# A softplus sum moved from VectorE to TensorE in a fused convolution and selective-scan kernel

## The reference

```python
xh = silu(causal_conv_k2(xh, conv_w, conv_b))
x_dbl = xh @ W_x                      # 8 columns for dt, 16 for B, 16 for C
dt = softplus(dt_low @ W_dt + b_dt)   # L x 256
h = exp(dt_t[..., None] * A) * h + dt_t[..., None] * B_t[:, None, :] * x_t[..., None]
y = einsum('bdn,bn->bd', h, C_t)      # + xh * D, then * silu(z), then @ W_out
```

## Time and profile before

| | us |
|---|---|
| median of 3 runs | 13842.76 |
| lowest, highest | 13840.99, 13844.69 |
| the profiled execution | 13837.79 |
| its span | 13836.0 |

### The profile page before, as it was taken

How to read it: one execution, slowest core, us unless ns; L and a number is a source line. 1 busy time by engine, 2 the same in 40 slices (tenths; PEclk the granted TensorE clock), 3 DMA queues, 4 the chain that set the end, 5 groups by cost and what they waited for, 6 DMA issues and landing times.

```text
span 13836.0 us, 170380 instructions
## 1 busy us (share of the span) xinstructions
PE 10079.9 (73%) x34752; PEld 2897.7 (21%) x34752; DVE 13466.6 (97%) x12084; ACT 12104.2 (87%) x24809; POOL 13246.6 (96%) x3076
## 2 busy tenths in 40 slices
PE   6777777777777777777777777777777777777776
PEld 1222222222222222222222222222222222222221
DVE  7999999999999999999999999999999999999999
ACT  7888888888888888888988888888898888888888
POOL 6999999999999999999999999999999999999999
PEclk8888888888888888888878888788888888888887
DMA  6667676666766676666667666666666666666665
GB/s 146 161 154 161 155 163 156 158 157 157 164 156 160 152 163 158 160 157 156 158 159 164 153 163 151 163 159 156 161 153 163 156 161 156 160 156 163 158 155 128
DMA packets 1195180, 2175.99 MB, mean 157 GB/s; under 512 B 152321, under 2 KB 161594, under 8 KB 1194042
## 3 DMA queue, kind: packets, MB, share of 16 engines
q1 hardware_dynamic: 1192762, 2164.07, 66.7%
q10 hardware_dynamic: 1280, 0.02, 0.0%
HBM read 1811.17 MB, written 352.32 MB: 156 GB/s over the span
## 4 chain that ended last, share of the span: by engine, by line
POOL 53%; issue 32%; DVE 6%; ACT 5%; PE 1%; DMA 1%; SPq 0%; POOLq 0%; ACTq 0%; DVEq 0%
POOL hq L1064 38%; POOL dbx L1054 15%; DVE hq L946 4%; ACT ps_a L640 2%; DVE dbx L929 1%; ACT dbx L654 1%; DMA b_rep<-bc_d 0%; DMA dt_d<-dt 0%; DVE pp L905 0%; ACT xh L600 0%; ACT L600 0%; ACT L765 0%; PE ps_acc L456 0%; DMA dtx_d<-sp 0%; POOLq L1063 0%
## 5 line engine op out<-in xcount | busy, mean ns | idle before, releaser
L1064 POOL TENSOR_TENSOR hq<-hq,c_rep 128x2048 f32<-128x2048 f32 x2048 | 9251.0, 4535 | 468.8 <-ACT carry L659 465.0
L946 DVE TENSOR_TENSOR_SCAN hq<-ps_a,dbx 128x512 f32<-128x512 f32 x8192 | 9443.6, 1207 | 128.8 <-ACT dbx L654 47.2
L640 ACT ACTIVATE ps_a<-dt_rep,A_neg 128x512 f32<-128x512 f32 x8192 | 5625.2, 687 | 1294.7 <-DVE hq L946 1231.5
L1054 POOL TENSOR_TENSOR dbx<-dtx_rep,b_rep 128x2048 f32<-128x2048 f32 (+1 forms) x1024 | 4082.1, 3986 | 99.1 <-DMA dtx_rep<-dtx_d 89.1
L654 ACT ACTIVATE dbx<-ps_a,dbx,carry 128x1 f32<-128x1 f32 x7168 | 2504.9, 349 | 240.2 <-POOL dbx L1054 140.4
L929 DVE TENSOR_TENSOR dbx<-dtx_rep,ps_b 128x2048 f32<-128x2048 f32 (+1 forms) x1280 | 2626.7, 2052 | 9.5 <-PE ps_b L444 9.3
L456 PE MATMUL ps_acc<-hq,dsum 128*32 128x512 f32 x16384 | 2334.0, 643 | 292.6 <-POOL hq L1064 292.6
L382 PE MATMUL pp<-sq,w_b1T 128*128 128x512 f32 x512 | 531.1, 1141 | 1608.7 <-ACT sq L579 1608.7
L444 PE MATMUL ps_b<-dbl,bsel 41*128 41x512 f32 x2560 | 1587.3, 703 | 153.3 <-DVE dbx L929 97.7
L400 PE MATMUL pp<-x,W_taps 128*128 128x512 f32 x768 | 693.3, 1002 | 895.2 <-DVE x L900 531.4
L456 PEld LDWEIGHTS ps_acc<-hq,dsum 128*32 128x32 f32 x16384 | 355.9, 111 | 1865.7 <-issue 1046.5
(11 more groups left out here) (123 smaller groups left out, 10466.4 us busy)
## 6 DMA issues: line engine op xcount, KB each, us to landing
dtx_rep<-dtx_d SPq DMA_DIRECT2D x2048, 256.0 KB, 5.4
dt_rep<-dt_d SPq DMA_DIRECT2D x2048, 256.0 KB, 6.3
c_rep<-bc_d SPq DMA_DIRECT2D x1024, 256.0 KB, 4.7
xr<-in_x SPq DMA_DIRECT2D x704, 256.0 KB, 10.9
b_rep<-bc_d SPq DMA_DIRECT2D x2048, 64.0 KB, 5.5
dtx_d<-sp SPq DMA_DIRECT2D x256, 512.0 KB, 2.8
dt_d<-dt SPq DMA_DIRECT2D x256, 512.0 KB, 6.1
xin<-in_x SPq DMA_DIRECT2D x256, 256.0 KB, 10.2
```

Source lines behind the costliest of these rows:

```text
L640: A(ps_a[:, BANK[i], :], dt_rep[:, q // NQ, g, :], ACT.Exp, scale=A_neg[:, q // NQ, q % NQ, g:g + 1]).then_inc(exp_done, 1)
L946: v.tensor_tensor_scan(hq[:, q % HQ, g, :], ps_a[:, BANK[i], :], dbx[:, slot(q), g, :], 0.0, ALU.mult, ALU.add).then_inc(scan_done, 1)
L1054: g.tensor_tensor(dbx[:, slot(q), m:, :], dtx_rep[:, d, m:, :], b_rep[:, q % NQ // 2, :].unsqueeze(1).to_broadcast([P, DG - m, T]), ALU.mu ...
L1064: g.tensor_tensor(quad, quad, c_rep[:, c % 2, q % NQ, :].unsqueeze(1).to_broadcast([P, DG, T]), ALU.mult).then_inc(cmul_done, 1)
```

## The change

The addition that ends softplus is taken from DVE and done by PE, by products with the identity that accumulate into the same two banks of `pp`. `W_dt` and the bias row are halved once at the start, so that `pp` holds v/2; ACT writes |v|/2 to `sp`; `Exp` with scale -2 and `Ln` write to `dt`, which is free until `evac_dt` writes it; and v/2 + |v|/2 + ln(1 + exp(-|v|)) is the sum of `pp`, `sp` and `dt`. `step_sum` adds `sp` (k = 0, after `Abs`) and `dt` (k = 1, after `Ln`). The wait of `evac_dt` for the store of the `dt` of the chunk before goes to `Exp`. `step_dt` and `step_sum` come ahead of `sum_states` within a slot. In slots: `evac_dbl` 9 to 8, softplus on ACT 12, 13, 14 to 11, 12, 13, `pool_part` 10, 11 to 14, 15; on PE `step_sum` in 12 and 14, convolution 11, 12, 13 to 13, 15, 16.

```diff
-PE_CONV = (11, 12, 13)
+PE_STEP = (12, 14)
+PE_CONV = (13, 15, 16)
-ACT_XZ, ACT_DBL, ACT_SP, ACT_DT, ACT_OUT = 5, 9, (12, 13, 14), 17, 23
+ACT_XZ, ACT_DBL, ACT_SP, ACT_DT, ACT_OUT = 5, 8, (11, 12, 13), 17, 23
-POOL_CHUNKS, POOL_SLOTS, ATT_CHUNK = (1, 2, 3, 4), (10, 11), CH - 4
+POOL_CHUNKS, POOL_SLOTS, ATT_CHUNK = (1, 2, 3, 4), (14, 15), CH - 4
...
+            def step_sum(b, c, k):
+                pe.wait_ge(sp_done, 3 * (b * CH + c) + (1, 3)[k])
+                for d in range(DI):
+                    last = mm(pp[:, d, :], w["ident"][:], (sp, dt)[k][:, d, :], start=False, stop=True, skip_group_check=True)
+                if k:
+                    last.then_inc(step_done, 1)
...
+                    if c + 1 < end:
+                        if u == PE_DT:
+                            step_dt(b, c + 1)
+                        for k in range(2):
+                            if u == PE_STEP[k]:
+                                step_sum(b, c + 1, k)
                     if g == 2:
                         if s >= 2:
                             sum_states(b, c, s - 2)
...
-                        if u == PE_DT:
-                            step_dt(b, c + 1)
...
-                        A(sp[:], sp[:], ACT.Exp, scale=-1.0).then_inc(sp_done, 1)
+                        if not (isinstance(b, int) and b * CH + c == 0):
+                            act.wait_ge(dt_out, 16 * (b * CH + c))
+                        A(dt[:], sp[:], ACT.Exp, scale=-2.0).then_inc(sp_done, 1)
-                        A(sp[:], sp[:], ACT.Ln, bias=1.0).then_inc(sp_done, 1)
+                        A(dt[:], dt[:], ACT.Ln, bias=1.0).then_inc(sp_done, 1)
...
             def evac_dt(b, c):
                 act.wait_ge(dtx_done, b * CH + c + 1)
-                if not (isinstance(b, int) and b * CH + c == 0):
-                    act.wait_ge(dt_out, 16 * (b * CH + c))
                 A(dt[:], pp[:, 0:2, :], ACT.Copy).then_inc(dt_done, 1)
...
+            v.tensor_scalar(w["wdt"][:], w["wdt"][:], 0.5, None, ALU.mult)
...
-            def softplus(b, c):
-                dve.wait_ge(sp_done, 3 * (b * CH + c + 1))
-                v.scalar_tensor_tensor(pp[:, 0:2, :], pp[:, 0:2, :], 0.0, sp[:], ALU.max, ALU.add).then_inc(step_done, 1)
...
-                            softplus(b, c + 1)
                             dt_x(b, c + 1)
```

More of the change, by code:

```diff
@@ L521, in _ @@
             step_dt(0, 0)
+            step_sum(0, 0, 0)
+            step_sum(0, 0, 1)
             for kw in (1, 0, 2):
@@ L1017, in _ @@
             add_input(0, 0)
-            softplus(0, 0)
             dt_x(0, 0)
```

## The result

The changed kernel takes 13,870.8 us (median of 20 runs, 13,842.0 to 13,899.3) against 13,841.8 us for the kernel before (20 runs, 13,839.6 to 13,845.9): ratio 1.0021, 95% interval 1.0015 to 1.0027. It is slower by 0.2%, 29 us, where 13,753 was forecast and the range ended at 13,840. Its executions also spread over 57 us, those of the kernel before over 6. And at its ends the spread goes with the clock: the two executions with a granted TensorE clock of 0.851 took 13,842 and 13,843 us, the three at 0.850 took 13,868 to 13,869, the two at 0.847 took 13,888 and 13,899; the thirteen at 0.848 and 0.849 took 13,861 to 13,887, in no order.

The account below looks back on a forecast made before the run. POOL bounds the middle chunks; DVE counts in chunk 5 and at the image end. Terms of -1.3 - 0.9 - 2.1 + 1.2 = -3.1 us an image, less givebacks, were taken as -90 us: 13,753; range 13,670 to 13,833, with rival 2 to 13,840.

Parts of the forecast that it names:

- DVE's addition: Removing DVE's softplus addition advances `dt_x` 0.9 us a chunk; POOL idle falls 0.9 us in chunk 5, 2.1 at image end.
- T: Moment in a chunk when POOL's first `dbx` product ends; scan 4 on DVE cannot begin before it.
- the rule of the Trainium skill: Highest-occupancy engine is the bottleneck, here DVE; by it all 313 us would come off, against 90 by the rows.
- The additions on TensorE: Two identity additions a chunk on TensorE, 1.95 us each, 1000 us in all; cost zero for what queues behind.
- The first rival: DVE is the bound throughout, so all 312.8 us are gained: 13,530 us; chance 5%.
- the second (additions too late): `dt_x` starts as late as before; chunk 5 and image end gain nothing: about 13,840 us; chance 14%.
- `Abs` ahead of the carry copy: ACT's `Abs` before the copy of carry 2: new POOL idle 0.4 us in chunks 5, 6, 7; 1.2 an image.
- `pool_part` out: `pool_part` leaves ACT slots 10 and 11: carry copy 0.3 us sooner in chunks 1 to 4, 1.3 us an image gained.
- One copy of `dbl` in twelve late gives back about 0.5 us an image: ACT's copy waits for slow `x_dbl` products: 7 chunks times 0.93 us times 8%, 15 us in all.
- the third rival: Slow clock reaches `x_dbl`, ACT waits in its `dbl` copy, POOL behind: 14,040 us; no gain from a third of chunks; 10%.
- its bad end, 13,833: Range's worst case: 0.9 us of POOL idle in three chunks, nothing from `pool_part`; -0.3 us an image, -9 us.
- errs towards too small a gain: TensorE pauses less, so more runs at 2.4 GHz; moved the forecast from about -80 to -90 us.

Follow-up runs that it names:

- with the clock kept: Half of the first z product repeated on TensorE: kernel before without DVE's addition (max(v, 0) left out) 13,738.7 us; changed kernel 13,796.1 us.
- the repeat: The changed kernel measured once more, unaltered, beside the kernel before on one chip: 13,861.1 us against 13,838.6, ratio 1.0018.

## Why the prediction was wrong, by its steps

**DVE's addition, 3.0 us an image (0.9 in chunk 5 and 2.1 at the end of an image), 93 us.** Right in size for the addition alone: 101 us with the clock kept, and POOL's idle time in the chunks 5 fell from 58.0 to 27.6 us there. In the changed kernel the end of the image gave 1.9 us in the image shown, and `dt_x` starts 21.8 us after T in chunk 7 on average where it was 22.7, the 0.9 us of the sum. Its chunk 5 gave nothing (64.1 us, and 68.8 with the clock kept). Moving `pool_part` alone had raised that idle time to 72.3 us, and `Abs` ahead of the copy added 19.8 at a place where there was none: the terms of the sum were not independent. The middle chunks are POOL's, and the rule of the Trainium skill that was set against the rows (Perfetto Trace Analysis, Identifying the Most-Contended Engine) would have given 313 us; the runs decide for the rows.

**The additions on TensorE, 1.95 us each, and nothing for what queues behind.** 2.0 us measured; ACT waited for the convolution's result 5.9 us in all, in two waits. The first rival did not occur, nor did the second (additions too late) in most chunks of the changed kernel; a late `dt_x` is what the two kernels with the copy of `dbl` in slot 9 have.

**The first step that failed: `Abs` ahead of the carry copy, 0.4 us in chunks 5, 6 and 7, against `pool_part` out, 1.3 us gained.** The forecast's net of the two is -0.1 us an image, 3 us gained. With the clock kept the changed kernel gains 44 us where DVE's addition alone gives 101, so all else in the change costs 57 us. The 0.4 was right for chunk 7 (0.37). But with the clock kept POOL stands as long in chunks 2 to 4 (0.37 us), with `pool_part` gone from there, and 0.62 in chunk 5; and `pool_part` out was worth 21 us, not 1.3 x 31 = 40. What I did not do was ask what a copy without slack does to every other wait of ACT. In the trace of before a slow product made a middle chunk 0.5 us longer, in the changed kernel 1.4: there the copy had slack behind it.

**The second step that failed: "One copy of `dbl` in twelve late gives back about 0.5 us an image".** Two numbers in it. The share of slow `x_dbl` products was taken from the kernel before, 8%, although the same text said in the third rival that DVE's lead lengthens the pause that causes them; it became 18%, and the kernel without the addition shows that the lead alone does it (62, from 21). And the price, 0.93 us, was ACT's wait; a slow chunk was 1.4 us longer. With 47 of them that is 66 us, not 15, and the changed kernel with the clock kept confirms it (66 to 73). In all: 101 gained, 57 lost, 66 to 73 lost, which makes the 22 to 29 us measured; against the terms of the forecast the first step was off by 60 us and this one by 51 to 58. Why an execution of the median is 29 us longer than the one traced stays open, for the repeat's trace has 48 slow products and is 13 us longer. The range left this term out: its bad end, 13,833, counts no slow product at all. The sentence that what is least certain "errs towards too small a gain (TensorE pauses less, so more runs at 2.4 GHz)", which took another 10 us off, had the sign wrong: TensorE had more work and a higher mean clock (0.851 against 0.815), but a longer pause at the one place that mattered.

**The third rival** named place and mechanism, and its sign, "ACT waiting for `x_dbl` in its copy", is what the trace shows (60.9 us). It got 10%, and its point of no gain, a third of the chunks, was too far off. At 1.4 us a chunk and 18% of the chunks it takes 2 us an image, and with the order on ACT at a loss of 57 us where the forecast had 3 gained, that was enough.

## What to carry to other kernels

When an instruction goes ahead of another on an engine, don't price it by its length alone: count the slack of what now stands behind it, for a wait of that engine that was covered before is paid in full from then on (two instructions in the other order: 13,861 to 13,718 us). When an engine gains lead, look for the pause that grows where another engine meets it, above all on TensorE, whose products behind such a pause ran at half the clock here. A share read off the kernel before is no forecast of a share after if the change moves its cause. And two gains that lean on the same place are not to be added: moving `pool_part` used up lead that the gain in chunk 5 was counted on.

## What the runs showed of the hardware

Pauses of TensorE of 1.2 us and more in front of the second z product were enough for the `x_dbl` product, three groups of products later, to take 2.77 us in place of 1.91. Twice the product that suffered was not the one looked at: filling that pause with the selection moved the slow clock to `dt`. The length of the pause matters but does not decide alone. In the changed kernel all 47 slow `x_dbl` products follow one of at least 1.2 us and none of the 196 shorter ones has a slow product behind it, yet 13 of the 60 long ones have none either; in the kernel before only 3 of 20 pauses that long do. By chunk, 26 of 32 chunks 3 have a slow `x_dbl` product (mean pause 1.30 us) and no chunk 7 (1.04). And a fast `x_dbl` product does not mean that the clock held. Chunk 7 of the image shown, on TensorE:

```profile
7335.35 1.12 PE L431 MATMUL pp<-x,Wz 128*128 128x512 f32 x2 [1.51 <-ACT xh L614]
...
7338.45 1.91 PE L417 MATMUL pp<-xh,w_Wx 128*40 128x512 f32 x4
...
7343.68 2.08 PE L461 MATMUL ps_acc<-xh,D_diag 128*128 128x512 f32 x2
```

After a pause of 1.51 us `x_dbl` is fast, and the product with D some 8 us later takes 2.08 us where it took 1.13 in chunk 3; the granted clock is 0.50 from 7343.6 to 7345.7. The additions come later by it, and `dt_x` begins at 7352.10, 22.8 us after T, as late as in the kernel before. What else decides where the slow stretch falls was not tried.

The Trainium skill (TensorE: Matmul & The Clock Gate, HAM oscillation) says that recurring waits can bring the slow clock back in every turn of a loop; the dt product with the copy of `dbl` in slot 9, at 682.1 / 256 = 2.66 us a chunk on average against 502.7 / 256 = 1.96, agrees for 186 of the 256 chunks. Half a product of 512 columns thrown away, 0.5 us of work, kept `x_dbl` at 1.91 us in all 256, in three kernels. And a kernel whose executions had agreed within 6 us spread over 57, the fastest at the highest mean granted clock and the slowest at the lowest.
